# A fused attention and FFN kernel: x1 as the last work of slot 3, LayerNorm's column arithmetic on GpSimd, the largest of h per quarter, h scaled in the next step's slot 0

## The reference

```python
x = x + xattn(layernorm(x), ctx)      # x (4, 1024, 256), ctx (4, 154, 192), 16 heads of 64
x = x + ffn(layernorm(x))             # float32 throughout

# xattn: q = xn Wq, k = ctx Wk, v = ctx Wv; softmax(q k^T / 8) v; @ Wo + bo
# ffn, hidden size 704:
def fp4_linear(x, w): return fp4_quant_dequant(x) @ fp4_quant_dequant(w).T
h = silu(fp4_linear(x, w_gate)) * fp4_linear(x, w_up)
return fp4_linear(h, w_down)
# fp4_quant_dequant: blocks of 16 along the last dimension, scale = max|x| / 6,
# each value rounded to the FP4 grid 0, 0.5, 1, 1.5, 2, 3, 4, 6 times its scale
```

## Time and profile before

| | |
|---|---|
| time before, median of 3 runs | 984.9 us (982.71 to 985.96) |
| the profiled execution's own time | 986.75 us |
| its span, first to last instruction | 984.9 us |
| busy: PE, DVE, ACT, POOL | 87%, 77%, 54%, 54% |
| mean granted TensorE clock | 0.973 of full |

### The profile page before, as it was taken

How to read it: one execution, slowest core, us unless ns; L and a number is a source line. 1 busy time by engine, 2 the same in 40 slices (tenths; PEclk the granted TensorE clock), 3 DMA queues, 4 the chain that set the end, 5 groups by cost and what they waited for, 6 DMA issues and landing times.

```text
span 984.9 us, 21389 instructions
## 1 busy us (share of the span) xinstructions
PE 857.0 (87%) x6254; PEld 812.8 (83%) x6254; DVE 757.5 (77%) x2176; ACT 534.0 (54%) x1879; POOL 529.5 (54%) x677
## 2 busy tenths in 40 slices
PE   4786789999999999989989999989999999999874
PEld 3666789988888998888978888889888888888863
DVE  5857788877778888867878888876877888887762
ACT  4454455556565555556555555556555555655520
POOL 2545666554535656545554656554553656555651
PEclk9888999999999999999999999999999999999986
DMA  7101000001010000001000000001000000000000
GB/s 215 39 11 49 7 17 13 22 13 44 7 33 17 13 23 11 21 14 39 12 28 23 12 22 12 21 8 33 23 7 23 12 18 12 16 11 12 7 11 11
DMA packets 19869, 23.13 MB, mean 23 GB/s; under 512 B 2642, under 2 KB 18234, under 8 KB 19770
## 3 DMA queue, kind: packets, MB, share of 16 engines
q1 hardware_dynamic: 19770, 21.94, 7.2%
HBM read 17.74 MB, written 4.19 MB: 22 GB/s over the span
## 4 chain that ended last, share of the span: by engine, by line
PE 63%; DVE 21%; issue 8%; ACT 4%; POOL 2%; DMA 1%; DVEq 1%; SPq 0%; POOLq 0%; ACTq 0%
PE ps_g L1015 10%; PE ps_q L937 8%; PE ps_s L975 8%; PE ps_t L985 5%; PE ps_o L998 5%; PE ps_o L1000 5%; PE ps_o L999 5%; DVE negmax L782 3%; DVE pT_lo L637 3%; PE ps_m L865 3%; PE ps_g L900 3%; PE ps_m L1025 3%; PE ps_m L1027 2%; PE ps_m L1026 2%; DVE scales L667 2%
## 5 line engine op out<-in xcount | busy, mean ns | idle before, releaser
L472 POOL TENSOR_TENSOR probs<-probs,rsum 128x308 f32<-128x308 f32 x256 | 180.0, 703 | 284.2 <-DVE rsum L746 283.6
L610 ACT ACTIVATE probs<-ps_s,negmax 128x154 f32<-128x154 f32 x512 | 194.7, 386 | 229.4 <-DVE negmax L782 228.2
L998 PE MATMUL ps_o<-B_sb,pT_lo 128*128 128x256 f32 x640 | 183.6, 287 | 38.5 <-DVE x_both L804 33.9
L782 DVE TENSOR_REDUCE negmax<-ps_s 128x2 f32<-128x308 f32 x256 | 121.3, 474 | 78.4 <-PE ps_s L975 76.6
L1000 PE MATMUL ps_o<-B_sb,pT_hi 128*128 128x256 f32 x640 | 181.2, 283 | 0.0
L999 PE MATMUL ps_o<-B_sb,pT_hi 128*128 128x256 f32 x640 | 180.9, 283 | 0.0
L998 PEld LDWEIGHTS ps_o<-B_sb,pT_lo 128*128 128x128 f32 x640 | 121.7, 190 | 45.3 <-issue 42.9
L637 DVE TENSOR_TENSOR pT_lo<-ps_t,pT_hi 128x256 fp32r<-128x256 f32 (+1 forms) x256 | 122.7, 479 | 42.6 <-ACT pT_hi L514 37.4
L985 PE MATMUL ps_t<-ident,probs 128*128 128x128 f32 x640 | 115.0, 278 | 35.9 <-DVE pT_lo L637 35.3
L1015 PE MATMUL ps_g<-WGU,xqT_hi 128*128 128x352 f32 x512 | 136.6, 349 | 3.5 <-DVE B_sb L637 1.9
L514 ACT ACTIVATE pT_hi<-ps_t 128x256 fp32r<-128x256 f32 (+1 forms) x256 | 111.4, 435 | 29.1 <-PE ps_t L985 22.7
(11 more groups left out here) (149 smaller groups left out, 2236.7 us busy)
## 6 DMA issues: line engine op xcount, KB each, us to landing
xa<-in_x_dram SPq DMA_DIRECT2D x33, 128.0 KB, 2.1
xr<-in_x_dram SPq DMA_DIRECT2D x32, 128.0 KB, 2.0
out_dram<-y_xn SPq DMA_DIRECT2D x32, 128.0 KB, 1.7
W_sb<-in_L_xattn_Wk_dram SPq DMA_DIRECT2D x4, 512.0 KB, 4.4
W_sb<-in_L_xattn_Wv_dram SPq DMA_DIRECT2D x3, 512.0 KB, 3.6
probs<-in_L_xattn_Wq_dram SPq DMA_DIRECT2D x1, 1024.0 KB, 7.0
Wo_sb<-in_L_xattn_Wo_dram SPq DMA_DIRECT2D x1, 1024.0 KB, 6.6
VT<-in_ctx_dram SPq DMA_DIRECT2D x1, 384.0 KB
```

What stands on the lines that cost most here:

```text
L472: pool.tensor_tensor(unit, unit, rsum[:, 2 * u:2 * u + 2].unsqueeze(2) .to_broadcast([P, 2, M]), ALU.mult).then_inc(norm_p, 1)
L610: ins = act.activation(probs[:, h, 0:M], ps_s[k % 2][:, s * M:(s + 1) * M], ACT.Exp, bias=negmax[:, h:h + 1], accum_out=sums[:, h:h + 1])
L782: dve.tensor_reduce(negmax[:, 2 * k:2 * k + 2], ps_s[k % 2][:, 0:UM].rearrange("p (h m) -> p h m", h=2), AX_X, ALU.max, negate=True).then_ ...
L998: pe.matmul(ps_o[:, 0:C], lo[:, j, :], w[:, 0:C], start=first, stop=False)
```

## The change

Four edits. x1 moves from the middle of slot 4 to the end of slot 3 on DVE, and the copy into y on ACT from slot 3 to slot 2. `stats` ends with bn_aggr; `rstd` on POOL adds EPS and negates the mean itself. The largest of h is taken per quarter, in slots 4 to 7, behind the slot's other work on h and x. The scaling of h leaves slot 7 and stands in the next step's slot 0, ahead of power. Semaphore counts follow (3 instead of 5 per LayerNorm, 9 instead of 6 per hidden tile), those lines are left out:

```diff
-            def rstd(ve, rs, nm, ready, done, before):
+            def rstd(mv, rs, nm, ready, done, before):
 
                 pool.wait_ge(*ready)
-                pool.tensor_tensor(rs[:, :], ve[:, :], pow_arg[:, :], ALU.pow).then_inc(done, 1)
-                pool.wait_ge(done, before + 1)
-                pool.tensor_tensor(nm[:, :], nm[:, :], rs[:, :], ALU.mult).then_inc(done, 1)
-
-            pool.wait_ge(pow_p, 1)
+                pool.tensor_tensor(rs, rs, mv[:, 1:2], ALU.add).then_inc(done, 1)
+                pool.tensor_tensor(nm, mv[:, 0:1], minus, ALU.mult).then_inc(done, 1)
+                pool.wait_ge(done, before + 2)
+                pool.tensor_tensor(rs, rs, pow_arg, ALU.pow).then_inc(done, 1)
+                pool.wait_ge(done, before + 3)
+                pool.tensor_tensor(nm, nm, rs, ALU.mult).then_inc(done, 1)
...
-                    if down and k == 3:
+                    if down and k == 2:
                         at = pair - 2 + par
                         act.wait_ge(x1_v, d + 1)
                         if some(at):
...
-            def stats(src, st, mv, ve, nm, ready, v, before):
+            def stats(src, st, mv, rs, ready, v, before):
 
                 dve.wait_ge(*ready)
-                dve.bn_stats(st[:, :], src).then_inc(v, 1)
+                dve.bn_stats(st, src).then_inc(v, 1)
                 dve.wait_ge(v, before + 1)
-                dve.memset(ve[:, :], EPS).then_inc(v, 1)
-                dve.bn_aggr(mv[:, :], st[:, :]).then_inc(v, 1)
-                dve.wait_ge(v, before + 3)
-                dve.tensor_scalar(nm[:, :], mv[:, 0:1], -1.0, None, ALU.mult).then_inc(v, 1)
-                dve.tensor_tensor(ve[:, :], mv[:, 1:2], ve[:, :], ALU.add).then_inc(v, 1)
+                dve.memset(rs, EPS).then_inc(v, 1)
+                dve.bn_aggr(mv, st).then_inc(v, 1)
 
...
                     if turn_at(t, k, 1) is not None:
                         chunk_lo(turn_at(t, k, 1))
                     if before and k == 4:
-                        dve.wait_ge(o_mm, PAIRS * (e + 1))
-                        dve.wait_ge(xr_p, e + 1)
-                        if some(d + 1):
-                            dve.wait_ge(y_a, d + 1)
-                        elif not some(e):
-                            dve.wait_ge(raw_mm, RAW_T[3])
-                        dve.tensor_tensor(x1[1 - par], xr[1 - par][:, :], ps_o[:, 0:C], ALU.add).then_inc(x1_v, 1)
                         if some(e):
                             dve.wait_ge(xln2_a, e)
-                        stats(x1[1 - par], st2, mv2, ve2, nm2, (x1_v, e + 1), ln2_v, 5 * e)
+                        stats(x1[1 - par], st2, mv2, rs2, (x1_v, e + 1), ln2_v, 3 * e)
                     if gate and 3 <= k < Q + 3:
                         silu(f, k - 3)
                     if own and ahead and k == 2:
@@ -812,11 +807,14 @@
                     if gate and 3 <= k < Q + 3:
                         hidden(f, k - 3)
                     if down and k == 0:
+                        if some(d):
+                            dve.wait_ge(hqT_mm, 2 * d)
+                        scaled(hn[:, 0:F], eh[:, 0:F], hri[:, :], hq_v, 9 * d + 3)
                         if gate:
                             dve.wait_ge(xq_p, 4 * f + 4)
-                        power(hn[:, 0:F], hc[:, :], (hq_v, 6 * d + 4), hq_v)
+                        power(hn[:, 0:F], hc[:, :], (hq_v, 9 * d + 7), hq_v)
                     if down and k == 1:
-                        rounder(hc[:, :], hq_v, 6 * d)
+                        rounder(hc[:, :], hq_v, 9 * d + 3)
                     if raw_at(t, k, 1) is not None:
                         chunk_divide(raw_at(t, k, 1))
                     if raw_at(t, k, 0) is not None:
@@ -829,9 +827,18 @@
                         fp4_scales(xri[:, :], xsc[:, :], xri[:, :], xq_v, 6 * e)
                         dve.wait_ge(xq_v, 6 * e + 3)
                         dve.tensor_scalar(xri[:, :], xri[:, :], TIES_DOWN, None, ALU.mult).then_inc(xq_v, 1)
-                    if gate and k == 6:
-                        dve.wait_ge(h_v, Q * (f + 1))
-                        largest(eh[:, 0:F], hri[:, :], hq_v)
+                    if before and k == 3:
+                        dve.wait_ge(o_mm, PAIRS * (e + 1))
+                        dve.wait_ge(xr_p, e + 1)
+                        if some(d + 1):
+                            dve.wait_ge(y_a, d + 1)
+                        elif not some(e):
+                            dve.wait_ge(raw_mm, RAW_T[3])
+                        dve.tensor_tensor(x1[1 - par], xr[1 - par][:, :], ps_o[:, 0:C], ALU.add).then_inc(x1_v, 1)
+                    if gate and 4 <= k < Q + 4:
+                        q = k - 4
+                        dve.wait_ge(h_v, Q * f + q + 1)
+                        largest(eh[:, q * QF:(q + 1) * QF], hri[:, q * QB:(q + 1) * QB], hq_v)
                     if before and k == 6:
                         if down:
                             dve.wait_ge(hq_p, 3 * d + 2)
@@ -842,10 +849,7 @@
                     if gate and k == 7:
                         if some(f):
                             dve.wait_ge(hq_p, 3 * f)
-                        fp4_scales(hri[:, :], hsc[:, :], hri[:, :], hq_v, 6 * f)
-                        if some(f):
-                            dve.wait_ge(hqT_mm, 2 * f)
-                        scaled(hn[:, 0:F], eh[:, 0:F], hri[:, :], hq_v, 6 * f)
+                        fp4_scales(hri[:, :], hsc[:, :], hri[:, :], hq_v, 9 * f + 3)
 
             schedule(dve, step)
```

More of the change, by code:

```diff
@@ L45, in xattn_ffn_kernel @@
     QF = F // Q
+    QB = QF // BLOCK
     CTX_T = -(-NB * M // P)
@@ L92, in xattn_ffn_kernel @@
         small = sb("small", [P, 24])
-        ln = [[small[:, 11 * i + a:11 * i + b] for a, b in ((0, 6), (6, 8), (8, 9), (9, 10), (10, 11))] for i in range(2)]
-        st1, mv1, ve1, rs1, nm1 = ln[0]
-        st2, mv2, ve2, rs2, nm2 = ln[1]
-        pow_arg = small[:, 22:23]
+        ln = [[small[:, 10 * i + a:10 * i + b] for a, b in ((0, 6), (6, 8), (8, 9), (9, 10))] for i in range(2)]
+        st1, mv1, rs1, nm1 = ln[0]
+        st2, mv2, rs2, nm2 = ln[1]
+        pow_arg, minus = small[:, 20:21], small[:, 21:22]
         x1_both = sb("x1_both", [P, 2, C])
@@ L430, in _ @@
                                base=0, pattern=[[-1, P]], channel_multiplier=1).then_inc(ident_p, 1)
-            pool.memset(pow_arg[:, :], -0.5).then_inc(pow_p, 1)
+            for v, value in ((pow_arg, -0.5), (minus, -1.0)):
+                pool.memset(v, value).then_inc(pow_p, 1)
             for v in (eh, y_xn, hn):
@@ L496, in step @@
                     if own and ahead and k == 3:
-                        rstd(ve1, rs1, nm1, (ln1_v, 5 * t + 20), ln1_p, 2 * t + 6)
+                        rstd(mv1, rs1, nm1, (ln1_v, 3 * t + 12), ln1_p, 4 * t + 12)
                     if before and k == 4:
-                        rstd(ve2, rs2, nm2, (ln2_v, 5 * e + 5), ln2_p, 2 * e)
+                        rstd(mv2, rs2, nm2, (ln2_v, 3 * e + 3), ln2_p, 4 * e)
                     if before and k == 6:
@@ L602, in step @@
                         elif q == 0:
-                            act.wait_ge(hq_v, 6 * f - 2)
+                            act.wait_ge(hq_v, 9 * f - 2)
                         act.wait_ge(gu_mm, Q * f + q + 1)
@@ L615, in step @@
                     if before and k == 5:
-                        act.wait_ge(ln2_p, 2 * e + 2)
+                        act.wait_ge(ln2_p, 4 * e + 4)
                         if some(e):
@@ L696, in layer_norm1 @@
                     dve.wait_ge(xln1_a, n)
-                stats(xa[par][:, :], st1, mv1, ve1, nm1, (ld_xa[par], 16 * pairs), ln1_v, 5 * n)
+                stats(xa[par][:, :], st1, mv1, rs1, (ld_xa[par], 16 * pairs), ln1_v, 3 * n)
             for half in range(2):
```

9 lines of the change are left out of this document (5 added, 4 removed).

## The result

| | before | after |
|---|---|---|
| median | 983.94 us (982.71 to 985.96, 4 runs) | 932.4 us (930.46 to 934.21, 4 runs) |
| ratio | | 0.947, 95% interval 0.944 to 0.951 |
| profiled execution, own time | 986.75 us | 934.21 us |
| mean granted clock | 0.973 | 0.978 |

The change brings 51.5 us. The forecast was 954.0 with a range of 944 to 970, a gain of 31; the direction was right, the size was outside the range. The median before is that of four runs here, 983.94 us, where the prediction had three and 984.9.

A forecast was written before the change was run, and what follows sets the result against it. PE, busy 87% of the span and waiting on DVE for x1 and pT_lo, was taken as the bound. 19 x 1.16 + 12 x 0.75 = 31.0 us off 984.9 made 953.9, forecast as 954 us, range 944 to 970.

The forecast's parts named there:

- The stall's price: Slot 4, PE waiting for x1 before attend: 1.47 us or 1.15 us by step, mean 1.31, to be gained.
- no change: Rival: slots 5 to 7 are the real bound, each microsecond gained at x1 returns in slot 7; 984 us, chance 0.05.
- step A: The par 1 step, x1 at 597.50 before, attend stall 1.47 us; B is the par 0 step, x1 at 622.23, 1.15 us.
- There I take 0.75, for want of a row (bounds 0 and 1.3): Net gain in us assumed for each of about 12 steps that make K, V and B for the next batch.
- The plain steps' 1.16: Net gain per steady tile in us: 1.26 less 0.10 for the scaling, counted for 19 tiles.
- +0.3 and -0.55 in the chain: DVE, largest of h per quarter: slot 5's quarter adds 0.3 us, slot 6's replaces the whole and saves 0.55.
- 0.25 in A and 0.16 in B: Up to slot 7's turn: 0.25 us of x1's gain given back in step A, 0.16 more gained in the par 0 step.
- give-back at the head of the chain in A: Slot 5, step A: DVE's negmax only 0.99 us earlier of 1.47, since pT_hi and hqT_hi wait on ACT behind LayerNorm 1's output.
- I take 0.1 us a tile: Scaling of h in slot 0 delays q_lo, so PE stalls at slot 1's q product; bounds 0 and 0.8 us.
- by itself: Column arithmetic on POOL, slots 2 and 4: not on PE's path by itself, but lets slots 0 to 2 run late harmlessly.
- more than that: Rival: slot 7's stalls fall too, as small prices in DVE's chain are lower; 1.5 us a tile, 938 us, chance 0.10.
- Collision: Rival, slots 0 and 1: scaling or power waits about 0.7 us for a POOL instruction, or POOL's for it; 971 us, chance 0.19.

The follow-up runs named there:

- x1 alone: Kernel before with one edit: x1 at the end of slot 3 and the copy into y in slot 2; 943.5 us, ratio 0.961.
- x1 and quarters: Kernel before with two edits: x1 early and largest of h per quarter, column arithmetic on DVE and scaling in slot 7 as before; 936.6 us, ratio 0.951.
- scaling alone: Kernel before with one edit: scaling of h moved to the next step's slot 0; 991.7 us, ratio 1.010.

## Why the prediction was off, point by point

**x1: right.** The stall's price, by the distance from where attend could have started, was 1.47 and 1.15 us, mean 1.31; the edit alone brings 1.22. The copy into y a slot earlier costs nothing that shows; no run moves it without x1. The rival "no change", by which each gain at x1 returns in slot 7, falls: 1.22 alone, 1.23 in company, and 0.30 of 1.47 given back in a step A.

**The failed step, and most of the miss: "There I take 0.75, for want of a row (bounds 0 and 1.3)" for the setup steps.** Measured 1.81, above even the upper bound; x1 alone is 1.44 there and 1.57 when it alone is taken back. There was a row: 33.9 us in 28 waits is 1.2 a wait and nearly one for each of the 31 tiles, so the stall was in the setup steps too, at 1.14, 1.47 and 1.70 us. Only the last of these stood behind a split of B. Twelve steps at 1.06 us more are 12.7 us.

**The plain steps' 1.16 against 1.65** are the other part, 19 x 0.49 = 9.3 us. Together 22.0; the profiled time came out at 934.21 where the same sum gave 955.7, 21.5 lower. That the two agree so closely is partly luck: every fourth setup step holds a loop's boundary, and these three gained 1.58, 3.35 and -0.44 us, not 1.81. In the plain steps four terms were mis-sized. In the order x1, quarters, column arithmetic, scaling the prediction had 1.06 + 0.20 + 0 - 0.10 = 1.16, and the windows have 1.22 + 0.32 + 0.10 + 0.01 = 1.65:

- The quarters: +0.3 and -0.55 in the chain, 0.25 in A and 0.16 in B, measured 0.42 to 0.43 where slot 4's quarter costs nothing, and 0.32 directly behind x1. The rows were read by duration, and a chain on one engine goes by starts. In the kernel before the whole takes 0.89 us, but the instruction behind it starts 0.80 later; the quarter takes 0.33 and gives way after 0.24, or 0.28 in slot 6. That is 0.24 added and 0.52 taken away. The chain from the reduction of xn to pT_lo was 607.52 - 602.97 = 4.55 us and is 574.51 - 570.34 = 4.17, so 0.38 shorter. The remaining 0.12 lies between silu's and the reduction's start in slot 6 (0.74 before, 0.62 after), and the prediction had no term for it. The whole had to wait for the quarter of h made just ahead of it: it starts at 606.12, and that quarter ends at 605.74 + 0.34 = 606.08. Slot 6 now reduces the quarter made in slot 5 and starts at 573.62, before the one ahead of it ends (573.36 + 0.34 = 573.70). This is read from the traces and from the waits in the diff; no run changes it alone.
- x1, by the give-back at the head of the chain in A: of x1's 1.47 us negmax of slot 5 was to keep 0.99. It went from 4.40 us after attend could start (600.99 - 596.59) to 3.21 (568.36 - 565.15), so it keeps 1.19. The mechanism was right as far as it went: LayerNorm 1's output on ACT stands in front of pT_hi and hqT_hi, and hqT_lo on DVE starts at 567.89, behind hqT_hi's end at 567.36 + 0.49 = 567.85. But there too I added durations, 0.59 and 0.38, where ACT's starts are 0.50 and 0.26 apart. And DVE's own work, which the prediction did not sum, is just as long: pT_lo at 567.57 gives way after 0.32, at 567.89 as well, with no idle time shown. For that reason slot 4's quarter, which the prediction put at nothing because a wait for scores stood behind it, costs 0.24 in A (3.45 for 3.21) as long as the pair is on DVE.
- The column arithmetic: nothing, measured 0.10. It gives back what slot 4's quarter takes, as the kernel "x1 and quarters" shows.
- The scaling: "I take 0.1 us a tile", measured 0.00 in company. The 0.23 that it costs alone comes by another way than I worked out, through LayerNorm's addition in slot 2, and the second edit removes that. I had costed the column arithmetic at nothing "by itself", with slots 0 to 2 able to run late without harm. The second half of that holds for slots 0 to 2 and should have carried the 0.1 away.

**The rival "more than that"** had a good part of the mechanism (reductions that cost less than taken, the stall of slot 7 falling as well) and 938 us as its full size. It came true beyond that, since its 1.5 us a tile was 1.65 and 1.81. Its other reason, LayerNorm 1's output starting earlier, did not come: that output starts 1.44 us behind the place where attend could start before, and 1.45 after. It said nothing of the setup steps, where most of the miss lies.

**What the profile was to show:** no PE wait on x1 (one is left, of 1.2 us, for the first tile), no one-column DVE instruction over 0.2 us, reductions of 11 blocks at 0.34 (0.32 to 0.33, once 0.57), no wait at slot 1's q products (PE's five waits for q_lo all lie before 40 us): all so. Slot 7's turn in A was to wait 0.2 to 0.3 us longer; it lost its wait, and a smaller one stands in slot 6. Pairs were to take 48.8 us and take 47.8. "Collision" didn't happen: all scalings of hn take 0.88 to 0.91 us but one of 1.10, all powers 0.53 but one of 0.88. The changed kernel's scaling and power in slot 0, on DVE:

```profile
555.45 0.88 DVE L683 SCALAR_TENSOR_TENSOR hn<-eh,scales 128x704 f32<-128x704 f32 x1
556.37 0.53 DVE L689 TENSOR_SCALAR hc<-hn 128x704 uint32<-128x704 uint32 x1
```

and POOL's product on xn, which had been beside the scaling in slot 7:

```profile
552.87 0.62 POOL L449 TENSOR_TENSOR y_xn<-y_xn,scales 128x256 f32<-128x256 f32 x1
```

Neither of these two DVE instructions met one of POOL's. The rule of the Trainium skill ("SBUF — State Buffer", section "Who interferes with whom"), that such instructions and GpSimd's take turns, holds here: its case is the 1.33 us for one column in scaling alone, which ends with POOL's subtraction. It spoke against the scaling's new place, and where it struck was two slots further on.

## What to carry to other kernels

Sum a chain on one engine by the distance from start to start of its instructions, not by their durations: here that turns 0.25 us into about 0.3 and 0.99 into 1.19. Look also at what an instruction had to wait for: a quarter made one slot ago is ready, the one made just now is not, and that was another 0.12. Before a bound is taken "for want of a row", divide the total of the waits by their count: 33.9 us in 28 waits, in a program of 31 such places, says that the stall is everywhere. And an edit that costs something alone may cost nothing beside another that removes what it ran into, so a small edit is judged in the company that it will have.
